# A turned picture stored through a scratch of its own, gathered in rows of 96, with other heads and variances

## The reference

```
x = x + layer(group_norm(x))                              # four times, l = 0..3
layer:  xn = layer_norm(x)                                 # over channels; not in layer 3
        left, right = (xn @ Wl) * sigmoid(xn @ Wlg), (xn @ Wr) * sigmoid(xn @ Wrg)   # with masks in 0, 1, 3
        t[i,j,d] = sum_k left[i,k,d] * right[j,k,d]        # layers 2, 3: sum_k left[k,j,d] * right[k,i,d]
        out = (layer_norm(t) * gate) @ Wout                # gate = sigmoid(xn @ Wog); in 1 and 3 the gate comes last
```

## Time and profile before

| what | us |
|---|---|
| median of 3 runs (lowest, highest) | 1524.15 (1522.71, 1531.39) |
| the profiled execution | 1531.67 |
| its span | 1529.5 |
| TensorE, VectorE, ScalarE, GpSimd busy in the span | 1282.1, 1041.8, 962.0, 543.4 |
| mean granted TensorE clock | 0.948 |

### The profile page before, as it was taken

One profiled execution on the slowest core, in us unless ns is written; L12 is line 12 of the kernel. 1 busy time (PEld: TensorE's weight loads), 2 busy tenths in 40 slices (PEclk: granted clock), 3 DMA queues, 4 the chain that ended last, 5 costly groups with the idle time before them and its releaser, 6 DMA issues. The chain is left out here.

```text
span 1529.5 us, 43851 instructions
## 1 busy us (share of the span) xinstructions
PE 1282.1 (84%) x12950; PEld 765.9 (50%) x12950; DVE 1041.8 (68%) x2976; ACT 962.0 (63%) x2093; POOL 543.4 (36%) x490
## 2 busy tenths in 40 slices
PE   0899998787789998989941999999789677799898
PEld 0455554444345455755521666667455333367455
DVE  7577774299789996219950788831499788821587
ACT  0577774489577774129940888831599688822575
POOL 0455551055456563005530666610156200000355
PEclk9899999899899999999975899999899899999999
DMA  8011113467533332896667333359689444369798
GB/s 275 27 52 46 51 51 111 114 202 225 169 101 103 106 115 72 254 286 177 195 152 188 103 115 113 108 174 300 180 262 278 154 141 138 129 185 307 212 291 258
DMA packets 206501, 249.31 MB, mean 163 GB/s; under 512 B 29024, under 2 KB 196320, under 8 KB 206432
## 3 DMA queue, kind: packets, MB, share of 16 engines
q1 hardware_dynamic: 206432, 248.42, 53.1%
HBM read 139.83 MB, written 108.53 MB: 162 GB/s over the span
## 5 line engine op out<-in xcount | busy, mean ns | idle before, releaser
L989 DVE SCALAR_TENSOR_TENSOR lr<-ps,mask,act_out 128x128 f32 (+5 forms) x1152 | 276.3, 310 | 61.7 <-ACT act_out L739 55.6
L1153 POOL TENSOR_TENSOR rstd<-ve,half_col 128x6 f32<-128x6 f32 x144 | 190.2, 1321 | 259.1 <-DVE ve L962 225.4
L511 PE MATMUL ps<-w_parts,val 64*128 64x256 bf16 (+1 forms) x2112 | 222.6, 304 | 47.4 <-DVE lr L989 41.9
L1196 POOL TENSOR_TENSOR new_ring<-val,lr 128x384 f32<-128x384 f32 x96 | 103.4, 1078 | 409.5 <-issue 325.0
L1186 POOL TENSOR_TENSOR val<-act_out,gate_ring 128x384 f32<-128x384 f32 x96 | 118.4, 1233 | 247.2 <-ACT act_out L817 231.1
L739 ACT ACTIVATE act_out<-ps 128x384 f32<-128x384 f32 x384 | 174.9, 481 | 34.2 <-PE ps L511 16.7
L783 ACT ACTIVATE in_ring<-ps 128x768 f32<-128x768 f32 (+1 forms) x64 | 51.8, 810 | 184.0 <-PE ps L579 161.9
L511 PEld LDWEIGHTS ps<-w_parts,val 64*128 64x128 bf16 (+1 forms) x2112 | 90.5, 111 | 133.3 <-DVE lr L989 94.7
L1085 DVE TENSOR_TENSOR sq_low<-sq 128x384 bf16<-128x384 f32 x192 | 120.1, 625 | 52.9 <-ACT sq L796 52.8
L621 PE MATMUL ps<-in_ring,k 128*128 128x384 f32 x288 | 134.5, 555 | 20.1 <-DMA in_ring<-t_scratch 19.7
L715 ACT ACTIVATE cen<-ps,gn 128x384 f32<-128x384 f32 x144 | 83.6, 581 | 104.1 <-PE ps L466 101.5
(11 more groups left out here) (101 smaller groups left out, 2574.8 us busy)
## 6 DMA issues: line engine op xcount, KB each, us to landing
gate_scratch<-gate_ring SPq DMA_DIRECT2D x192, 192.0 KB, 2.2
gate_ring<-gate_scratch SPq DMA_DIRECT2D x96, 384.0 KB, 3.7
in_ring<-x_scratch SPq DMA_DIRECT2D x144, 192.0 KB, 2.4
lr<-x_scratch SPq DMA_DIRECT2D x72, 384.0 KB, 4.5
in_ring<-t_scratch SPq DMA_DIRECT2D x144, 192.0 KB, 3.3
x_scratch<-new_ring SPq DMA_DIRECT2D x48, 384.0 KB, 2.9
t_scratch<-in_ring SPq DMA_DIRECT2D x48, 384.0 KB, 3.4
lr<-x SPq DMA_DIRECT2D x6, 1536.0 KB, 15.3
```

Source lines behind the costliest of these rows:

```text
L511: mm = nc.tensor.matmul(banks[h][:, :, 0:P], moving(x, s)[half(h), N * r:N * r + P], proj_weights(w, h)[:, 0:2 * P], start=start, stop=sto ...
L989: ins = nc.vector.scalar_tensor_tensor(out5[:, h, lo // 2:hi // 2, :, m], ps[:, 4 + 2 * r + h, lo:hi].rearrange("p (a e) -> p a e", e=2), ...
L1153: nc.gpsimd.tensor_tensor(rstd[:, s % 2, :], ve[:, s % 2, :], half_col[:, :], ALU.pow)\
```

## The change

1. **The turned picture.** A new DRAM tensor `turned_scratch` [h, h2, channel, row, 96] takes `turned` in two parts, 4 tiles' worth (8 rows) and the rest. SyncE stores the first part, ScalarE's queue the second; each as two transfers of all 128 partitions. In layer 2 `gather` loads two tiles at a time in rows of 96 floats and puts them together in natural order; `keep` writes the pair to `x_scratch` for the residual. `column_parts` and `x_parts` go. VectorE's wait for the stores moves behind its prologue.
2. **Heads of the second halves.** The first two gate pairs are loaded at group 12 of phase_b1. Residual loads of groups 14 and 15 come after the first t loads and have their own semaphore. The prologue of TensorE takes another order, with two `keep_clock` matmuls fewer.
3. **Variances of layer 0's phase_b2** are float32 matmuls on `sq`; `square_low` goes there.
4. **Layer 3's phase_a.** The high part is read as the upper two bytes of `xn` in place (`xn_high`); ScalarE's `high` goes, `plain` is issued last in the step, and `low` is a plain subtraction.

```diff
-EARLY = 8
+EARLY = 4
+LATE = 14
+    turned_dram = nc.dram_tensor("turned_scratch", [2, 2, C, HALF, HALF], F32).ap()
+        xn_high = xn[:, :, :].bitcast(BF16).rearrange("p s (f e) -> p s f e", e=2)[:, :, :, 1]
+        def turned_rows(h2, first, behind):
+            return (turned_dram[:, h2, :, first:behind, :],
+                    turned[:, HALF * h2 + first:HALF * h2 + behind, :])
...
+                def gather(n, s):
+                    for h in range(2):
+                        rows = turned_dram[h].rearrange("h2 c j i -> (h2 c) j i")[:, bass.ds(ROWS * n, 2 * ROWS), :]
+                        slot = in_ring[:, s:s + 2, :].rearrange("p a (r i) -> p (a r) i", r=ROWS)
+                        sp.dma_start(slot[:, :, HALF * h:HALF * h + HALF], rows).then_inc(in_loaded[s], 16)
+                def keep(n, i, s):
+                    sp.wait_ge(in_loaded[s], in_count(l) + 32 * (i + 1))
+                    sp.dma_start(two_tiles(scratch, n), in_ring[:, s:s + 2, :]).then_inc(natural_stored[s // 2], 16)
+                def step_gathering(n, i, s, ahead):
+                    if s % 2 and ahead >= RING + lead - 1:
+                        sp.wait_ge(used, l * TILES + n + lead + 1)
+                        sp.wait_ge(natural_stored[s // 2], 16 * (i + 2))
+                        gather(n + lead + RING - 1, s - 1)
+                    sp.wait_ge(a_gate, l * TILES + n + 1)
+                    sp.dma_start(gate_dram[n, :, :], gate_ring[:, s, :]).then_inc(gate_stored[s], 16)
+                    if s % 2 and ahead >= RING + 1:
+                        keep(n + RING + 1, i + (s + 5) // RING, (s + 1) % RING)
...
+                if l == 2:
+                    for n in range(0, RING, 2):
+                        gather(n, n)
+                    for n in range(0, RING, 2):
+                        keep(n, 0, n)
+                    sp.wait_ge(turned_stored[1], 16 * 2)
+                    for n in range(0, RING, 2):
+                        sp.wait_ge(used, l * TILES + n + 2)
+                        sp.wait_ge(natural_stored[n // 2], 16)
+                        gather(RING + n, n)
+                    keep(RING, 1, 0)
+                    over_tiles(sp, step_gathering, 2 * RING)
+                    return
...
-                    for n in freed_slots(l, g) if l else []:
+                    if l == 2 and g == 0:
+                        for pair in range(PAIRS):
+                            sp.wait_ge(natural_stored[pair], 16 * TURNS)
+                    for n in freed_slots(l, g) if l and g < LATE else []:
+                        load_residual(l, n, res_loaded)
+                    if g == LATE - 2:
+                        for s in range(RING):
+                            sp.wait_ge(gate_stored[s], (l + 1) * 16 * TURNS)
+                        for n in range(0, RING, 2):
+                            load_gate(l, n, n)
...
                 for n in range(0, RING, 2):
                     load_t(n, n)
-                    load_gate(n, n)
+                for g in range(LATE, GROUPS) if l else []:
+                    for n in freed_slots(l, g):
+                        load_residual(l, n, late_loaded)
...
-                    for part, tiles in enumerate((slice(0, EARLY), slice(EARLY, TILES))):
-                        for h in range(2):
-                            for h2 in range(2):
-                                rows = turned[C * h:C * h + C, h2 * HALF:(h2 + 1) * HALF, :]
-                                sp.dma_start(quarters[h, h2, :, tiles, :],
-                                             rows.rearrange("p (t r) i -> p t (r i)", r=ROWS)[:, tiles, :])\
-                                    .then_inc(turned_stored[part], 16)
-                    sp.wait_ge(turned_stored[0], 16 * 4)
+                    for h2 in range(2):
+                        sp.dma_start(*turned_rows(h2, 0, ROWS * EARLY)).then_inc(turned_stored[0], 16)
+                    sp.wait_ge(turned_stored[0], 16 * 2)
...
+                    if not ln and part == 0:
+                        return xn_high[:, s % 2, :]
...
-                    for z, x in zip(column_parts(l, ps[:, s % 2, 0:TILE]),
-                                    x_parts(l, in_ring[:, s, :]) if l else [x_all[:, n, :]]):
-                        mm = nc.tensor.matmul(z, w_centre[:, :], x, start=True, stop=True)
-                    mm.then_inc(a_z, 1)
+                    nc.tensor.matmul(ps[:, s % 2, 0:TILE], w_centre[:, :], in_ring[:, s, :] if l else x_all[:, n, :],
+                                     start=True, stop=True).then_inc(a_z, 1)
...
+                    if l == 0:
+                        pe.wait_ge(b2_sq, base + n + 1)
+                        for j in range(CHUNKS):
+                            mm = nc.tensor.matmul(ps[:, 6 + s % 2, 2 * j:2 * j + 2],
+                                                  sq[:, s % 2, P * j:P * j + P], k_sel, start=True, stop=True)
+                        mm.then_inc(b2_var, 1)
+                        return
...
-                for n in range(4):
-                    centre(n, 0, n)
+                centre(0, 0, 0)
+                centre(1, 0, 1)
                 keep_clock(4, 1)
                 variance(0, 0)
-                keep_clock(4, 1)
+                centre(2, 0, 2)
                 variance(1, 1)
                 spread(0, 0)
-                keep_clock(4, 1)
-                centre(4, 1, 0)
+                centre(3, 0, 3)
                 spread(1, 1)
                 variance(2, 2)
+                centre(4, 1, 0)
...
-                    if not ln and ahead >= 1:
-                        high(n + 1, (s + 1) % RING)
-                    if not ln and ahead >= 2:
-                        plain(n + 2, i + (s + 2) // RING, (s + 2) % RING)
                     if ln and ahead >= 1:
                         high(n + 1, (s + 1) % RING)
                     sigmoids(n, s, 0)
                     sigmoids(n, s, 1)
                     if ln and ahead >= 4:
                         centred(n + 4, s)
+                    if not ln and ahead >= 2:
+                        plain(n + 2, i + (s + 2) // RING, (s + 2) % RING)
...
                     turn(TILES - 1, RING - 1)
+                    act.wait_ge(b2_turned, TILES)
+                    for h2 in range(2):
+                        act.dma_start(*turned_rows(h2, ROWS * EARLY, HALF)).then_inc(turned_stored[1], 16)
...
-                if l == 2:
-                    for part in range(2):
-                        dve.wait_ge(turned_stored[part], 16 * 4)
...
+                        nc.vector.tensor_tensor(xn_parts[:, s % 2, 1, :], xn[:, s % 2, :], xn_high[:, s % 2, :],
+                                                ALU.subtract).then_inc(a_lo, 1)
...
                 if IN_PARTS[l]:
                     low(0, 0)
+                if l == 2:
+                    for part in range(2):
+                        dve.wait_ge(turned_stored[part], 16 * 2)
                 over_tiles(dve, step)
...
-                        for new, out, x in zip(column_parts(l, new_ring[:, s, :]),
-                                                 column_parts(l, ps[:, 4 + s % 2, 0:TILE]), res):
-                            ins = nc.vector.scalar_tensor_tensor(new, out, bias, x, ALU.add, ALU.add)
-                        ins.then_inc(b2_new, 1)
+                        if l and isinstance(n, int) and n == RING - 1:
+                            dve.wait_ge(late_loaded, residual_count(l, True))
+                        nc.vector.scalar_tensor_tensor(new_ring[:, s, :], ps[:, 4 + s % 2, 0:TILE], bias, residual_slot(l, n),
+                                                       ALU.add, ALU.add).then_inc(b2_new, 1)
...
-                    if ahead >= 4:
+                    if l and ahead >= 4:
                         square_low(n + 4, s)
```

More of the change, by code:

```diff
@@ L191, in t_tiles @@
             return t_dram(l).rearrange("c (h t f) -> h c t f", h=2, f=TILE)[:, :, bass.ds(n, 2), :]
-        def column_parts(l, tile):
-            if l != 2:
-                return [tile]
-            return [tile.rearrange("p (r h i) -> p h r i", h=2, r=ROWS)[:, h, :, :] for h in range(2)]
-        def x_parts(l, tile):
-            if l != 2:
-                return [tile]
-            return [tile.rearrange("p (h r i) -> p h r i", h=2, r=ROWS)[:, h, :, :] for h in range(2)]
         slots = lr[:, :].rearrange("p (a f) -> p a f", f=TILE)
@@ L217, in freed_slots, with residual_count @@
             return [n for n in pairs if n < TILES]
+        def residual_count(l, late):
+            return 16 * sum(len(freed_slots(m, g)) for m in range(1, l + 1) for g in range(GROUPS) if (g >= LATE) == late)
         def two_tiles(dram, n):
@@ L235, in plane_out, with in_count @@
             return main.rearrange("p (d q) -> p d q", q=N), tail.rearrange("p (d q) -> p d q", q=N)
-        def in_count(l):
-            return 16 * TURNS * (l - 1)
+        def in_count(l, s=0):
+            return 16 * TURNS * ((l > 1) + (l > 2) * (2 if s % 2 == 0 else 0))
```

(40 more changed lines are left out.)

27 lines of the change are left out of this document (14 added, 13 removed).

## The result

The changed kernel takes 1629.82 us (median of 4 runs, 1627.48 to 1630.74); the kernel before, beside it, 1525.41 (1522.71 to 1531.39). The ratio is 1.0676, interval 1.0642 to 1.0711: 104 us slower. The profiled execution took 1630.41 with a span of 1628.1; its mean granted TensorE clock is 0.917, against 0.948.

A forecast was written before the change was run, and what follows sets the result against it. No engine bounds the whole span; each stage has its own limit, and a 48 us store only moves data. +132 - 9 - 4 - 7 - 11 = +101; 1531.7 + 101 - 7.5 = 1625 us, range 1450 to 1660.

The forecast's parts named there:

- The store: Store of the turned picture before layer 2: 189 us at 25 GB/s per engine, first write into `lr` +128 us.
- two outermost pieces mean two engines: Store of the turned picture: a transfer dealt out by its outermost pieces occupies two engines; chance 0.63, range 1595 to 1660.
- the 14 us of the pipeline's start: Layer 2's start: hidden under the store; 14 us come back if early pieces pass as slowly as long ones.
- the rival with 16 engines: Store of the turned picture: all 16 engines work, 34 us, -54 in all, 1470 us; chance 0.30.
- Tile 4 and the late part, +4: Layer 2's projections: tile 4 is gathered only after the second part has landed, delaying TensorE's work: +4 us.
- Gathers and keeps, 0: Layer 2's projections: gathering two tiles and keeping them is covered by TensorE's work, cost 0.
- Layer 0's variances, -9: Layer 0's second half: float32 variances take L1085 from VectorE, -9 us, bounds 0 and -11.
- Layer 2's residual, -4: Layer 2's second half: residual in one instruction instead of two on VectorE, -4 us, bounds 0 and -10.
- Layer 3's projections, -7: Layer 3's projections: L748, 513 ns a tile, leaves ScalarE, -7 us, bounds 0 and -19.
- Heads, -11: Heads of the second halves: loads leave the front of t, 4 us each in layers 1 and 2; -11, bounds 0 and -18.
- first L621 two us sooner after its issue: Sign at the heads of the second halves: the first L621 comes two us sooner after its issue, the third four.
- the rival that I gave 0.04 and 1484: Layer 2's start with 16 engines: the early part starves beside the long pieces, 14 us return, 1484 us; chance 0.04.

The follow-up runs named there:

- e1_halves: The changed kernel with each store of the turned picture cut in two by h, 64 channels outermost: 1501.61 us, ratio 0.9826.
- e7_early_first: The changed kernel with ScalarE's queue issuing the late part only when the early part has landed: 1629.49 us, ratio 1.0661.
- e4_variances: The kernel before with layer 0's float32 variances alone: 1516.61 us, ratio 0.9924.
- e5_layer3: The kernel before with layer 3's projections alone, high part read in place: 1516.23 us, ratio 0.993.
- e3_wide: The changed kernel with scratch as [h2][h][channel], 128 outermost pieces a store, gathers of 64 partitions: 1483.81 us, ratio 0.9713.
- e12_before_two_queues: The kernel before with its own store issued by two queues, partitions 0 to 63 by ScalarE's, 64 to 127 by SyncE's: ratio 0.9911.
- e11_halves_at_once: e1_halves with the late transfers of partitions 64 to 127 on SyncE's queue: ratio 0.9826.

## Why the prediction was right, and where its terms were off

**The store.** The step on which all hung, that two outermost pieces mean two engines, is shown: 54 GB/s at a share of 0.13, 3.7 engines with four, and the whole loss gone in e1_halves. Its size was off twice, and by luck the errors cancel. The store took 177.7 us (779.9 to 957.6), not 189, because long pieces run at 27 GB/s on an engine and not 25.0. And the 14 us of the pipeline's start were not hidden. I had kept that for the range, and in the rival with 16 engines had argued "the 3,072-byte pieces are a queue of their own, against it"; a queue of its own doesn't help on an engine that serves both queues one piece each. First issue to first write grew by 129.7 us, where I had 128.

The rule of the Trainium skill that I had weighed (DMA: Bandwidth & Descriptors, Why a DMA increments its semaphore by 16 and not by 1) agrees with all three counts here, 2, 4 and 16. Its 27 GiB/s an engine (Specifications), 29 GB/s, is above the 27 GB/s measured.

**Tile 4 and the late part, +4.** Nothing of it: first write to first triangle product took 159.7 us before and 158.8 after. 129.7 - 0.9 is the 128.8 of the table. In e7_early_first, where the pipeline's start lies under the store, the term does show up: 163.6 us.

**Gathers and keeps, 0.** Right. In 1010 to 1110 TensorE is 95.64 of 100 busy; the DMA share rose to 0.55.

**Layer 0's variances, -9.** -8.6 by the stages, -12 (8 to 15) by e4_variances alone. ScalarE and TensorE became the bound together.

**Layer 2's residual, -4.** -4.6 by the stages; no run has this edit alone.

**Layer 3's projections, -7.** The term was too small: -11.9 by the stage, -11 by e5_layer3. The tile went from 2.78 to 2.56 us. Of L748's 0.513 us a tile I let the round of waits eat 0.36; it ate some 0.27, and 11.9 / 48 = 0.25 came back. What shrank is VectorE's wait for ScalarE's sigmoids (L739, after L792) at the product with the projection (L989, after L1046).

In the kernel before (1225 to 1325), and then after (1335 to 1435), by the view of waits (us in total, times, longest):

```profile
DVE lr L989 <- ACT act_out L739: 11.8, 27, 0.6
```

```profile
DVE lr L1046 <- ACT act_out L792: 3.0, 17, 0.2
```

**Heads, -11.** Wrong: 0. The step that failed is "Three or four loads ... leave the front (1.4 us each at 281 GB/s)". They stood in a wait that had to be waited anyway. I priced what was issued ahead of t and didn't look at what releases t. The promised "first L621 two us sooner after its issue" came to 0.95 in layer 3. Layer 0 loses 2.8 us, and the little that layers 1 to 3 gain is within the scatter of the traces: the sum is 0 (-1 to +5).

**The sum.** 128.8 - 8.6 - 4.6 - 11.9 = 103.7, and 104.4 by the medians. The forecast of 1625 against 1629.82 is thus nearer than its terms, and that is luck: heads 11 too much, layer 3 5 too little, store and tile 4 together 3 too much. One sum on record is off: the forecast's own range should start at 1625 - 27 = 1598 and not at 1595.

**The rivals.** All 16 engines at 1470: with the store of e3_wide the same edits give 1484, so that world was priced about right; it took another shape of scratch. The early part starved on two engines, and on all 16 as well: in e3_wide SyncE issues the first gather, which waits for it, at 801.1, and the store ends at 803.1, so the first write, at 820.1, is 17 us behind the store. That is the rival that I gave 0.04 and 1484. The mechanism is right; that the number fits to a microsecond is luck, since the heads that it counts on gave nothing.

## What to carry to other kernels

Before a large transfer, write down the outermost dimension of both sides as the instruction carries it. Here 64 and 128 kept all engines busy, 2 and 4 did not; merge or cut until it is like the first, and let one transfer span all 128 partitions. A small transfer that others wait for isn't safe on a second queue while long pieces run on the same engines. Before you pay for loads moved out of the way, look at what the waiting load is released by: if that is a landing and not the queue, nothing is gained, and loads moved forward may delay the stores that others need. And before you read an experiment by its time, look in its trace whether the condition that it was to make came about.

## What the hardware showed that I had not expected

- **64 partitions, half the rate.** With full DMA engines a store from 64 partitions ran at 210 GB/s in 768-byte pieces and 217 in 33,792-byte pieces, one from 128 partitions at 434. The Trainium skill (SBUF — State Buffer, Door 1: The DMA port swizzle) says that partitions 0 to 63 reach only 8 of 16 ports of 27.2 GB/s each; an estimate from its figures is 218 and 435, and these windows of the long pieces agree to 1%; over the whole stores, 780.6 to 825.2 in e1_halves and 780.8 to 803.1 in e3_wide, it is 210 and 411. It would have told me that the kernel before, too, ran at half rate there.
- **Two queues, both halves of the partitions.** In 768-byte pieces both halves at once gave 326 GB/s, one half at a time 210. The same page (Can I just issue two DMAs to hit both halves?) says no, +6%; e12_before_two_queues doesn't agree. e11_halves_at_once can't tell: its long pieces of the two halves went one after the other.
- **Turns by piece.** A queue with 3,072-byte pieces beside one with 33,792-byte pieces got 186 packets for 186, and so a twelfth of the bytes (0.57 of 6.78 MB). A store of 0.79 MB that lands in 18 us alone took 160 us beside it.
- **One engine** alone moved 27 GB/s, with pieces of 33,792 bytes.
